# A GRU with a convolution beside it: the convolution's banks stand beside steps 2 to 14 instead of 1 to 13

## The reference, cut to what matters

```python
def reference(x, cond_2048, L0_cond_b, L1_cond_W_ih, L1_cond_W_hh, L1_cond_b_ih, L1_cond_b_hh):
    # conv: causal, depthwise, padding K - 1 on the left, taps w[K, 1, D], plus b
    x = x + conv(x, cond_2048[:, None, :], L0_cond_b)
    h = cond_2048
    for t in range(64):
        i_r, i_z, i_n = split(x[:, t] @ W_ih + b_ih, 3)
        h_r, h_z, h_n = split(h @ W_hh + b_hh, 3)
        r, z = sigmoid(i_r + h_r), sigmoid(i_z + h_z)
        n = tanh(i_n + r * h_n)
        h = (1 - z) * n + z * h
        out[:, t] = x[:, t] + h
```

## Time and profile before

| | |
|---|---|
| median of 3 runs | 1212.7 us (1211.54 to 1214.32) |
| the profiled execution | 1213.68 us; its span 1211.9 us |
| PE busy with matmuls | 1179.8 us, 97% of the span |
| DVE, ACT busy | 558.5 us (46%), 466.6 us (39%) |
| DMA | 92.18 MB, mean 76 GB/s |
| granted TensorE clock, mean | 0.995 |

### The profile page before, as it was taken

How to read it: one execution, slowest core, us unless ns; L and a number is a source line. 1 busy time by engine, 2 the same in 40 slices (tenths; PEclk the granted TensorE clock), 3 DMA queues, 4 the chain that set the end, 5 groups by cost and what they waited for, 6 DMA issues and landing times.

```text
span 1211.9 us, 14952 instructions
## 1 busy us (share of the span) xinstructions
PE 1179.8 (97%) x5524; PEld 977.4 (81%) x5524; DVE 558.5 (46%) x942; ACT 466.6 (39%) x804; POOL 15.0 (1%) x20
## 2 busy tenths in 40 slices
PE   5989999989999999999999999999999999999997
PEld 4968878878888888888888888888888888888886
DVE  3737768766874434334333343333433334333333
ACT  4346656656663333233332333332333323333232
POOL 0300000000000000000000000000000000000000
PEclk9989999999999999999999999999999999999999
DMA  9978888788842011110111101111011110011100
GB/s 260 284 144 165 164 171 170 160 171 178 165 124 70 20 34 35 35 35 20 32 35 35 35 21 31 35 35 35 22 30 35 35 35 24 28 35 35 35 18 18
DMA packets 251906, 92.18 MB, mean 76 GB/s; under 512 B 176810, under 2 KB 246442, under 8 KB 249824
## 3 DMA queue, kind: packets, MB, share of 16 engines
q1 hardware_dynamic: 248332, 90.52, 32.3%
q10 hardware_dynamic: 3540, 1.22, 0.4%
HBM read 57.56 MB, written 34.14 MB: 76 GB/s over the span
## 4 chain that ended last, share of the span: by engine, by line
PE 91%; SPq 3%; DMA 3%; DVE 1%; ACT 1%; issue 0%; ACTq 0%; DVEq 0%
PE bank L818 82%; PE bank L841 3%; PE bank L807 2%; PE bank L773 2%; SPq L361 1%; DMA xres<-stage 1%; PE bank L842 1%; DMA early<-early_result 1%; SPq L372 1%; PE bank L794 1%; SPq L346 1%; DMA conv_b_rows<-in_L_cond_b_dram 0%; DMA x_unit<-in_x_dram 0%; SPq L417 0%; DMA h<-in_cond_dram 0%
## 5 line engine op out<-in xcount | busy, mean ns | idle before, releaser
L818 PE MATMUL bank<-w_ih_hi,xT_hi 128*128 128x512 f32 x768 | 309.2, 403 | 1.7 <-ACT bank L546 1.7
L818 PE MATMUL bank<-w_hh_hi,hT_hi 128*128 128x512 f32 x768 | 304.4, 396 | 0.0
L818 PE MATMUL bank<-w_hh_hi,hT_lo 128*128 128x512 f32 x768 | 300.6, 391 | 0.0
L818 PE MATMUL bank<-w_hh_lo,hT_hi 128*128 128x512 f32 x768 | 300.4, 391 | 0.0
L818 PE MATMUL bank<-w_ih_hi,xT_lo 128*128 128x512 f32 x768 | 300.3, 391 | 0.0
L818 PE MATMUL bank<-w_ih_lo,xT_hi 128*128 128x512 f32 x768 | 299.5, 390 | 0.0
L818 PEld LDWEIGHTS bank<-w_hh_hi,hT_lo 128*128 128x128 f32 x768 | 144.9, 189 | 31.3
L818 PEld LDWEIGHTS bank<-w_ih_hi,xT_lo 128*128 128x128 f32 x768 | 144.2, 188 | 31.8
L818 PEld LDWEIGHTS bank<-w_ih_hi,xT_hi 128*128 128x128 f32 x768 | 144.4, 188 | 28.8 <-ACT bank L546 1.5
L818 PEld LDWEIGHTS bank<-w_hh_lo,hT_hi 128*128 128x128 f32 x768 | 145.0, 189 | 28.0
L818 PEld LDWEIGHTS bank<-w_hh_hi,hT_hi 128*128 128x128 f32 x768 | 144.9, 189 | 28.1
(11 more groups left out here) (68 smaller groups left out, 888.9 us busy)
## 6 DMA issues: line engine op xcount, KB each, us to landing
x_unit<-in_x_dram SPq DMA_DIRECT2D x64, 256.0 KB, 4.5
out_dram<-outZ SPq DMA_DIRECT2D x256, 64.0 KB, 1.6
toep_ring<-kernel_parts SPq DMA_DIRECT2D x128, 96.0 KB, 2.9
xres<-stage SPq DMA_DIRECT2D x32, 384.0 KB, 4.5
xT<-xres SPq DMA_DIRECT2D x48, 256.0 KB, 2.7
early<-early_result SPq DMA_DIRECT2D x4, 1024.0 KB, 16.3
xT<-early SPq DMA_DIRECT2D x60, 64.0 KB, 1.9
w_ih_raw<-in_L_cond_W_ih_dram SPq DMA_DIRECT2D x12, 256.0 KB, 8.5
```

The costliest lines, as they stand in the source:

```text
L818: mm = nc.tensor.matmul(psum[:, :], a[:, rows], b[w][:, cols], start=False, stop=stop and n == 2, skip_group_check=True)
```

## The change

BULK_FIRST and BULK_LAST go from 1 and 13 to 2 and 14. With them move the 128 banks and all that hangs on them. At the end of step BULK_LAST the last stage store, the wait for the stage stores and the loads of x of steps 16 and 17 now stand ahead of the output of that step; x of step 18, which is loaded into the place that this output frees, stays behind it.

```diff
--- before.py
+++ after.py
@@ -14,7 +14,7 @@
 RING = 4
 EARLY = 16
 POINTS = 10
-BULK_FIRST, BULK_LAST = 1, 13
+BULK_FIRST, BULK_LAST = 2, 14
 
 
 def conv_residual_gru(
@@ -431,6 +431,12 @@
                     bulk(t, point)
                     if point == 1 and isinstance(t, int) and BULK_FIRST <= t <= BULK_LAST:
                         finish(t - 1)
+                if isinstance(t, int) and t == BULK_LAST:
+                    store_stage(NBANK * 2 // STAGE - 1)
+                    for n in range(2):
+                        sp.wait_ge(stage_stored[n], 32 * (PAIRS // STAGE // 2))
+                    for late in range(EARLY, t + RING):
+                        load_xT(late % RING, T - 1 - late)
                 if not isinstance(t, int) or t + 1 < BULK_FIRST or t >= BULK_LAST:
                     sp.wait_ge(outZ_ready, t + 1)
                     store_out(u, t)
@@ -438,11 +444,7 @@
                     if t + RING < EARLY and t + 1 < BULK_FIRST:
                         load_early_xT(t + RING)
                     if t == BULK_LAST:
-                        store_stage(NBANK * 2 // STAGE - 1)
-                        for n in range(2):
-                            sp.wait_ge(stage_stored[n], 32 * (PAIRS // STAGE // 2))
-                        for late in range(EARLY, t + RING + 1):
-                            load_xT(late % RING, T - 1 - late)
+                        load_xT(u, T - 1 - RING - t)
                     if t > BULK_LAST and t + RING < T:
                         load_xT(u, T - 1 - RING - t)
                 else:
```

## The result

The changed kernel takes 1201.9 us (median of 4 runs, 1200.2 to 1203.5) against 1213.5 (4 runs, 1211.5 to 1215.2): ratio 0.9904, 95% interval 0.988 to 0.9929, or -11.6 us where -11.4 had been forecast. The profiled execution took 1200.42 us, its span 1198.6, so the two profiles lie 13.3 apart. That the medians hit the forecast to 0.2 us is partly luck: the interval reaches from 8.6 to 14.6 us less, and the same kernel, run again in a later set (e5, 0.9884), gained some 14.

The account below looks back on a forecast made before the run. PE is busy nearly throughout, but SP's late single queue sets when stage stores land. Start -8.07, step 5 -4.05, step 8 +0.75, end 0 sum to -11.4: 1212.7 to 1201.3 us; own range 1200 to 1203, 8 in 10 1197.0 to 1206.0.

Parts of the forecast that it names:

- start: wait and half clock: Step 1: the first bank's 5.37 us wait for x_parts and 2.70 of half clock both go, -8.07.
- step 5, now 6: Late stage store: SP gains 3.3 us on PE, so PE's 2.25 wait and 1.80 half clock go, -4.05.
- step 8, now 9: SP stands 0.75 us further behind, the stage store is later and the step's loss grows to 5.5, +0.75.
- end of the convolution: Last stage store, x of step 16, bias: bias ready at 380.1, wanted at 380.43, cover 0.3 us, cost 0.
- Rival (e): First bank waits in step 2 as in step 1; could be a us, no change would need 8; 1%.
- SP at its gates: SP, late before, is level with PE at the fifth toep pair: would start at 114.8, gate 114.93.
- the two ways left open: From unit 2's x load, SP's stream is 5.86 us later if its gate wait counts, 4.95 if transfers drain meanwhile.
- What holds it up is the transfers: SP's unbroken issue stream is held up by transfers; DMA engines' share 1.03 from 172 to 178 us.
- rival (b): Middle stalls stay or step 8 costs more than step 5 saves: 1204.6, with half clock in step 8 1206.4; 20%.

Follow-up runs that it names:

- e1: The kernel before with only the convolution moved to steps 2 to 14, the old tail order kept; ratio 0.9924 to the kernel before.
- e2: The changed kernel with the convolution back at steps 1 to 13, so only the tail's order differs from the kernel before; ratio 0.9997 to it.
- e12: The changed kernel plus one unused 786 KB copy issued by SP at bank 12; ratio 0.9926 to the kernel before.
- e10: The changed kernel with each stage store issued two banks earlier in SP's queue, timed in the third set; ratio 0.9855 to the kernel before.
- e4: The changed kernel with each stage store issued two banks earlier in SP's queue, timed in the first set; ratio 0.9832 to the kernel before.
- e6: The changed kernel with the first 15 stage stores issued by ScalarE instead of SP, second set; ratio 0.9851 to the kernel before.
- e9: The kernel before, convolution not moved, with the first 15 stage stores issued by ScalarE instead of SP; ratio 0.9947 to the kernel before.
- e11: The changed kernel with the first 15 stage stores issued by ScalarE instead of SP, third set; ratio 0.9865 to the kernel before.
- e7: The kernel before, convolution not moved, with each stage store two banks earlier in SP's queue; ratio 0.9964 to the kernel before.
- e8: The changed kernel with stage stores two banks earlier and each step's output and early x four points later; ratio 0.9868 to the kernel before.

## Why the prediction was right, point by point

| term | predicted | measured (profiles) |
|---|---|---|
| start: wait and half clock | -8.07 | -8.14 |
| step 5, now 6 | -4.05 | -4.04 |
| step 8, now 9 | +0.75 | -1.11 |
| other steps (10, now 11) | 0 | -0.31 |
| end of the convolution | 0 | 0 |
| sum | -11.4 | -13.6; -11.6 by the medians |

**The start** was right in mechanism and size. The first bank had been put at 95.4 and its x_parts at 94.6; it stood at 95.68, and the two splits that DVE runs from 93.67 take 2.10 together, so the first ends near 94.7. No wait, no half clock. Rival (e) is out.

**Step 6** is right in this profile and the second of the changed kernel (0 and 0.15 lost), not in e1's, where 2.88 was lost: it starts at 176.84, 8.99 later than step 5 did, and the store came 5.67 later, so SP had gained 3.3, as forecast, and that clears a wait of 2.25. (In e1 the store stood at 182.14, 7.57 later than before: a gain of little more than 1.) DVE's wait went from 6.57 to 3.10, by 3.5.

**SP at its gates** is right. The fifth pair of taps was issued at 115.20, directly behind the end of bank 9 at 114.95 + 0.22 = 115.17, and the x load at 118.57, directly behind its split at 117.44 + 1.10 = 118.54:

```profile
114.95 0.22 PE L844 MATMUL bank<-x_parts,toep_ring 128*96 128x128 f32 x1
```

```profile
115.20 2.19 SPq L372 DMA_DIRECT2D toep_ring<-kernel_parts  x2
```

```profile
117.44 1.10 DVE L700 TENSOR_TENSOR x_parts<-x_unit,x_parts 128x512 fp32r<-128x512 f32 x1
```

Both gates held SP, so the shift came out at the upper of the two ways left open (5.83, bound 5.86), where the forecast took the middle, 5.4. That the store of step 6 then stood 5.67 - 0.31 = 5.36 later, as if 5.4 had been right, is luck: from the x load to that store the stream was half a us shorter than before.

**Step 9 is the term that was mis-sized.** The step of the prediction was "those 4.05 were time in which SP caught up: from there SP stands 4.05 - 3.3 = 0.75 further behind". That takes SP's stream to be of one length up to that store. By the stores for steps 6 and 9 (5 and 8 where the convolution starts a step earlier) it was 72.6 in before, 70.4 in after, 71.0 in the second profile of after, 73.0 in e1, 73.6 in e2 and 71.5 in e12. Had it been 72.6 in after, the store would have stood at 252.8 and not 250.6, 2.2 later, and with 2.2 more the loss is 5.8 where 5.5 had been forecast. So with the old length the accounting would come out, and the length is what failed; its range, 70.4 to 73.6, is what separates the first profile of after from the forecast. e1, with the same order up to step 14, shows the other end: a stream of 73.0 and 6.9 lost in step 9, half clock in it.

Why one execution's stream is shorter was not settled. e12 shows one thing that lengthens it, transfers under way. And one order stands out in the six profiles: where the step of the first store lost 0, 0.15 and 1.8 us the stream took 70.4, 71.0 and 71.5; where it lost 2.9, 4.1 and 5.9, it took 73.0, 72.6 and 73.6. If a stall lengthens the stream, SP doesn't catch up by the whole of it, as the prediction had it. But the long ones of e1 and e2 are also of one chip, and no run here tells which makes which.

**The end** is right: order alone nothing (e2), the move without it 3.64 and the half clock (e1). The cover was half a us and not 0.3 by the prediction's own terms: 378.1 to 378.2 and three times 0.60 is 379.9 to 380.0, not 380.1, against 380.43. That the prediction left the half clock out of the 3.6 cost nothing, as the case didn't come.

**"What holds it up is the transfers"** is upheld only in part. A burst of transfers does lengthen an issue (e12), but the mean share is the same without stalls (e10), and a different place in the queue, or another queue, takes the stalls away at the same bytes (e4, e6, e9 to e11). The 1.03 in the earlier trace rows is 6 us at one place and doesn't speak for the stretch.

**Half clock, rival (b)**, was a fair doubt. It came behind PE waits of 2.25 (before), 2.56 and 3.64 (e1) and 2.06 (e7), and not behind the 0.57, 1.09 and 0.96 of after. But the length of the wait alone doesn't tell: behind 2.03 (e8), 2.11 (e1) and 2.63 (e7) the clock stayed at 1.00. Step 9 had half clock in e1 and not in the two profiles of the changed kernel. The Trainium skill ("TensorE: Matmul & The Clock Gate", Part 1) says of a kernel's start that the number of slow matmuls varies between runs of one kernel; these waits in the middle, alike in length and not in what followed, go the same way.

**A version that beats both**: e10 and e11 take 1195.8 and 1196.7 us where before takes 1213.4; they can't be told apart (0.9855 and 0.9865, intervals overlapping). In the second set e6 was 5.1 us below the changed kernel on the same chip (1198.2 and 1203.3). Every step from 1 to 15 of e10 is within 0.04 us of its undisturbed length, so the middle has nothing more to give.

The 0.9 us of step 10, now 0.59 in step 11, were in no term.

Left open: what sets the length of SP's stream; when a wait of PE is followed by half clock; the two groups of times in the first four runs.

## What to carry to other kernels

When one queue issues everything in order, read at its gates how late it stands against the compute engine, and carry that lateness forward: a later start of the compute gives the queue a lead only down to its next gate, and a stall that goes in one place can return at the next one (e1) if the queue hasn't gained as much. Moving a late store ahead in such a queue makes what it overtakes late; where the queue is short of time throughout (e7) that eats much of the gain, where it has a little lead (e10) it takes all stalls away, and a second queue does so in both, but for 1.8 us in e9. Before a chain is moved next to the end of a phase, work out its cover: here it was half a microsecond, and the order that put an output ahead of the store (e1) cost 5.35 us.

## What the runs showed of the hardware

- An issue on SP is short or long by what is under way: two x loads of 256 KB took 1.85 and 2.07 us to issue in two profiles of the changed kernel, and 4.39 behind a copy of 786 KB that was itself issued in 0.61 (e12). In before such pairs took 4.36 to 4.53 directly behind a stage store that was itself issued in some 1.1.
- The DMA engines' mean share over 200 us was 0.82 to 0.83 with and without stalls, so a share below 1 did not mean that the queue had time left.
- A wait of PE can cost more than itself: in e1 the wait of 3.64 made step 15 longer by 5.35, with a granted clock of 0.50 behind it. Waits of 2.06, 2.25 and 2.56 were followed by half clock too, waits of 2.03, 2.11 and 2.63 were not.
